# A decoder block on one core: the first batch's context products of the fp8 attention, its input norm and two of its streams issued beside the last scan, and the output weight converted in the seven steps that follow

## The reference

```python
# state space layer, per batch; the norm of (x + this) is the input of the attention
zxbcdt = x @ W_in.T                       # z, x/B/C after a causal convolution, dt
Yd = einsum(M, xs); y = Yd + Yoff + D * xs
yn = rmsnorm(y * silu(z)) * norm_w
x = layernorm(x + yn @ W_out.T)

# fp8 attention layer, per batch
xn = layernorm(x) * ln_w + ln_b
q, qx, k, v = fp8(xn / in_scale) @ wq, wqx, wk, wv       # four "streams"
kx, vx = split(ctx @ w_kv_x)                             # the context products
q, qx, k, kx = per head layer norms
o = concat(softmax(q k) v, softmax(qx kx) vx)
x = layernorm(x + fp8(o / smooth) @ wproj)               # wproj: the output weight
```

## Time and profile before

| | us |
|---|---|
| median of 3 runs | 2132.15 |
| lowest and highest of the 3 | 2131.37, 2134.02 |
| the profiled execution | 2134.4 |
| its span, first to last instruction | 2132.6 |

### The profile page before, as it was taken

The page is one execution under the profiler, slowest core; times in us unless marked ns, Lnnn a source line. Parts: engine busy times, 40 slices in busy tenths (PEclk is TensorE's granted clock), DMA queues, the critical chain, the costliest instruction groups (busy, mean ns, idle before and its releaser), DMA issues.

```text
span 2132.6 us, 34976 instructions
## 1 busy us (share of the span) xinstructions
PE 1977.0 (93%) x9620; PEld 1278.7 (60%) x9620; DVE 1624.9 (76%) x3820; ACT 1392.8 (65%) x5294; POOL 1251.1 (59%) x1540
## 2 busy tenths in 40 slices
PE   7979999999999998799999858999999999999996
PEld 5636666666666666455554425666666666666664
DVE  7855676766776667689899836778888888888887
ACT  3555666666666666356765237777777777777774
POOL 0154445445545443388787924777777777777774
PEclk9999999999999999899999869999999999999998
DMA  6000000000000002100000020000000000000000
GB/s 230 1 18 6 3 4 3 2 2 5 2 2 2 2 0 85 69 3 28 20 21 20 0 74 16 3 4 6 6 6 5 6 5 5 8 5 6 3 3 8
DMA packets 30211, 37.37 MB, mean 18 GB/s; under 512 B 3472, under 2 KB 24464, under 8 KB 29456
## 3 DMA queue, kind: packets, MB, share of 16 engines
q1 hardware_dynamic: 30096, 36.11, 5.1%
HBM read 34.01 MB, written 2.10 MB: 17 GB/s over the span
## 4 chain that ended last, share of the span: by engine, by line
PE 61%; DVE 14%; ACT 11%; POOL 7%; issue 6%; DMA 0%; POOLq 0%; SPq 0%; ACTq 0%; DVEq 0%
PE fa_pJB L2003 5%; PE xa_pJB L736 5%; PE xa_pS L755 5%; PE xa_pO L830 5%; PE xa_pY L867 4%; PE fa_pS L2085 4%; PE xa_pJA L736 3%; PE fa_pO L2028 3%; PE fa_pJA L1983 3%; PE fa_pY L2042 3%; PE fa_pH L2134 3%; PE fa_pJB L1983 2%; POOL ssm_y L1387 2%; PE fa_pH L2101 2%; PE ssm_pX L1445 2%
## 5 line engine op out<-in xcount | busy, mean ns | idle before, releaser
L2160 ACT ACTIVATE fa_qT<-fa_pH,all_fa_head_vec 128x512 f32<-128x512 f32 x128 | 99.9, 780 | 172.0 <-PE fa_pH L2134 172.0
L1933 POOL TENSOR_TENSOR fa_rs<-fa_rs,all_minus_half 128x4 f32<-128x4 f32 x192 | 197.1, 1027 | 15.0
L2169 ACT ACTIVATE fa_pS<-fa_pS,fa_nb 128x128 f32<-128x128 f32 x512 | 183.9, 395 | 6.5 <-DVE fa_nb L2353 6.5
L1930 POOL TENSOR_TENSOR fa_rs<-fa_ms,all_eps5w 128x4 f32<-128x4 f32 x192 | 44.2, 230 | 228.8 <-ACT fa_q_junk L2153 127.0
L1387 POOL TENSOR_TENSOR ssm_y<-ssm_y,ssm_term 128x512 f32<-128x512 f32 x112 | 144.1, 1287 | 55.5 <-DVE ssm_term L1699 52.2
L2085 PEld LDWEIGHTS fa_pS<-fa_kT,fa_qT 128*128 128x128 f32 x1024 | 124.3, 191 | 65.8 <-ACT fa_qT L2160 58.8
L1958 POOL TENSOR_TENSOR fa_cat<-fa_ov,fa_om 128x512 bf16<-128x512 f32 x125 | 150.3, 1203 | 5.1
L2085 PE MATMUL fa_pS<-fa_kT,fa_qT 128*128 128x128 f32 x1024 | 148.2, 288 | 3.0 <-ACT fa_qT L2160 0.9
L1949 POOL TENSOR_TENSOR fa_ov<-fa_ob,fa_om 128x512 f32<-128x512 bf16 x125 | 144.3, 1154 | 0.9 <-DVE fa_om L2301 0.9
L2369 DVE TENSOR_TENSOR fa_qn<-fa_pJA,fa_rs 128x512 f32<-128x512 f32 x128 | 88.4, 691 | 73.4 <-POOL fa_rs L1933 73.3
L682 POOL TENSOR_TENSOR xa_rs<-xa_ms,all_eps 128x4 f32<-128x4 f32 (+1 forms) x65 | 13.1, 202 | 223.1 <-ACT xa_junk L906 223.1
(11 more groups left out here) (340 smaller groups left out, 5802.0 us busy)
## 6 DMA issues: line engine op xcount, KB each, us to landing
all_shared_weights<-in_fa_w SPq DMA_DIRECT2D x12, 512.0 KB, 3.7
fa_cat<-in_fa_wproj SPq DMA_DIRECT2D x8, 512.0 KB, 3.9
all_shared_weights<-in_xa_wq SPq DMA_DIRECT2D x1, 2048.0 KB, 13.8
xa_wo<-in_xa_wo SPq DMA_DIRECT2D x1, 2048.0 KB, 17.9
xa_ctxT<-in_ctxT SPq DMA_DIRECT2D x16, 128.0 KB, 2.1
all_shared_weights<-in_fa_wkvx SPq DMA_DIRECT2D x1, 2048.0 KB, 10.0
fa_ctxT<-in_ctxT SPq DMA_DIRECT2D x16, 128.0 KB, 2.2
out_x<-all_X SPq DMA_DIRECT2D x16, 128.0 KB, 1.7
```

Source lines behind the costliest of these rows:

```text
L1933: pool.tensor_tensor(rs[:, j % 2, cols], rs[:, j % 2, cols], env.mhalf[:, cols], ALU.pow)\
L2169: last = act.activation(four(pS[j % 2])[:, i, :], four(pS[j % 2])[:, i, :], ACT.Exp, bias=nb[:, j % 2, i:i + 1], accum_out=rsum[:, j % 2, ...
```

## The change

What the attention prepares for its batch 1 in steps 0 to 3 is issued from inside the scan, by functions `early(n)` that each engine of `fa` hands to `ssm`:

- PE: the context keys 0 and 1 behind the convolution of batch 16 (m = 15), the key transposes, both context value products and the transposes of `xn` among and behind the levels of batch 16 (m = 16).
- ACT: eight squares at the end of m = 15; `kT` twice, `v` twice and `lnT` at the end of m = 16.
- POOL: one power for both key blocks (128x8 in place of two 128x4) behind its `xd` work of m = 15; the power of `xn` between the sums of levels 3 and 4; the sum of the first stream in m = 17.
- DVE: the input norm and both `kn` between the terms of batch 16; the whole first stream and the second one up to `xm` in m = 17, ahead of the residual of batch 16.

Instead of the norm of batch 16, the first early piece waits for the last use of what the scan's inputs hold (`front_left`); SP loads the context of batch 1 behind the last level of batch 15 and the first two weight chunks behind `front_left`. With m = 0 the steps 0 to 3 of `fa` are gone and 4 to 7 stay (`REST`); the wait for the norm of batch 16 stands behind them, and ACT applies that norm in step 5. The eight weight chunks go to the steps 4, 5, 6 (one each), 7 (two), and 0, 1, 2 of m = 1 (one each), in the order `PROJ`; ACT writes a high part before `qT` and the squares of its step. Buffers are split and laid out anew so that what is used early lies in places that the scan has left.

```diff
+                    if m == B and l == 3:
+                        early(1)
...
                 pool_rms(m - 1)
+                early(2)
                 pool_norm(m - 1)
...
+            if m == B - 1:
+                early(0)
...
+                if m == B and n in (5, 6):
+                    early(n - 4)
...
+            if m == B - 1:
+                early(0)
+            if m == B:
+                early(3)
...
-            if m == B + 1:
-                normalised(m - 1)
-
+            if m >= B - 1:
+                early(m - (B - 1))
...
+        def last_batch_normalised():
+            act.wait_ge(s["shift_done"], now(B, 0))
+            act.activation(shift[:], shift[:], ACT.Copy, scale=-1.0).then_inc(s["shift_signed"], 1)
+            act.wait_ge(s["shift_signed"], now(B, 0))
+            act.activation(env.X[:, B - 1, :], norm.res[:, 0, :], ACT.Identity, bias=shift[:],
+                           scale=norm.rstd[:, 0, :]).then_inc(norm.x_done, 1)
...
+            if m == B + 1:
+                early(3)
             terms(0, 1)
+            if m == B:
+                early(0)
...
+            if m == B:
+                early(1)
...
+            if m == B:
+                early(2)
...
+    def front_left(eng):
+        for n in ("xs_ps", "bc_in", "z_in", "xs_in", "cbd_done", "own_done", "xdt_done"):
+            eng.wait_ge(s[n], now(B, 0))
+        eng.wait_ge(s["dec_late"], of_pair(B))
+        eng.wait_ge(level_ps, now(B - 1, 0, LEVELS, LEVELS - 1))
+        eng.wait_ge(low_done, len(chunks))
...
+    def scan_input_left(eng):
+        eng.wait_ge(level_ps, now(B - 1, 0, LEVELS, LEVELS - 1))
...
+    pJB, pH, pP, pJA = ps("pJB"), ps("pH"), ps("pP"), ps("pJA")
     pS = [ps("pS0"), ps("pS1")]
-    pH, pP, pO, pY = ps("pH"), ps("pP"), ps("pO"), ps("pY")
+    pY, pO = ps("pY"), ps("pO")
...
+    PROJ = [0, 1, 2, 6, 7, 3, 4, 5]
+    REST = range(4, UNITS)
+    PROJ_FIRST = ((), (), (), (), (0,), (1,), (2,), (3, 4))
+    PROJ_SECOND = ((5,), (6,), (7,), (), (), (), (), ())
...
-        steps(0, 0, False, True, False, False)
+        steps(0, 0, False, True, False, False, REST)
+        env.ssm_stage.left(eng)
...
+    def early_of(eng, pieces):
+        def early(n):
+            if n == 0:
+                env.ssm_front_left(eng)
+                eng.wait_ge(env.fa_ready, 1)
+            for piece in pieces[n]:
+                piece()
+        return early
...
-        env.ssm_stage.left(sp)
+        env.ssm_scan_input_left(sp)
         load(1, 1)
+        env.ssm_front_left(sp)
         load_proj(0)
         load_proj(1)
...
+        def first_keys():
+            pool.wait_ge(kk["squared"], at(1, 1, 4))
+            pool.tensor_tensor(rs[:, 0, :], ms[:, 0, :], env.eps5w[:, 0:2 * HG], ALU.add).then_inc(kk["eps"], 2)
+            pool.wait_ge(kk["eps"], at(1, 1, 4))
+            pool.tensor_tensor(rs[:, 0, :], rs[:, 0, :], env.mhalf[:, 0:2 * HG], ALU.pow).then_inc(kk["rstd"], 2)
+        def first_input():
+            pool.wait_ge(s["eps0_done"], at(1, 0, 1))
+            pool.tensor_tensor(rs0[:], mv0[:, 1:2], env.mhalf[:, 0:1], ALU.pow).then_inc(s["rs0_done"], 1)
+        def first_stream():
+            pool.wait_ge(sx["xm_done"], at(1, 0, 4))
+            pool.tensor_tensor(xv[:, STREAMS[0]], xb[:, STREAMS[0]], xm[:, STREAMS[0]], ALU.add)\
+                .then_inc(sx["x_added"], 1)
+        return early_of(pool, [[first_keys], [first_input], [first_stream]]), lambda: sequences(pool, steps, drain)
...
-        env.ssm_stage.left(pe)
-        pe.wait_ge(env.fa_ready, 1)
-        sequences(pe, steps, drain)
+        def context(bank, c, signal):
+            for k in range(KT):
+                last = pe.matmul(bank[:, :], ctxT[:, 1, k, :], w_kvx[:, k, c * 512:(c + 1) * 512],
+                                 start=(k == 0), stop=(k == KT - 1))
+            last.then_inc(signal, 1)
+        def first_products():
+            pe.wait_ge(ctx_in[1], 16)
+            context(pJB, 0, kk["ps"])
+            context(pJA, 1, kk["ps"])
+        def first_keys(n, bank):
+            pe.wait_ge(kk["scaled"], at(1, n, 4))
+            for i in range(HG):
+                last = pe.transpose(bank[:, i * P:(i + 1) * P], kn[:, i, :], env.ident[:])
+            last.then_inc(kk["T_ps"], 1)
+        def first_values(n, bank):
+            context(bank, 2 + n, v_ps)
+        def first_input():
+            pe.wait_ge(s["xn_done"], at(1, 0, 1))
+            pe.wait_ge(kk["T_in"], at(1, 0, 4))
+            for k in range(KT):
+                last = pe.transpose(pH[:, k * P:(k + 1) * P], xn[:, k * P:(k + 1) * P], env.ident[:])
+            last.then_inc(s["xn_ps"], 1)
+        early = early_of(pe, [[first_products], [lambda: first_keys(0, pH)],
+                              [lambda: first_keys(1, pP), lambda: first_values(0, pJB)],
+                              [first_input, lambda: first_values(1, pJA)]])
+        return early, lambda: sequences(pe, steps, drain)
...
-        def steps(m, side, attend, front, back, last_linear):
+        def proj_high(c):
+            act.wait_ge(wp_in[c % 2], 16 * (c // 2 + 1))
+            if c == 5:
+                env.ssm_out_left(act)
+            act.activation(w_proj[:, 0, 4 * PROJ[c]:4 * PROJ[c] + 4, :], wp_raw[:, c % 2], ACT.Copy)\
+                .then_inc(wp_high, 1)
...
+                for c in (PROJ_FIRST[j] if not attend else PROJ_SECOND[j]) if front and not back else ():
+                    proj_high(c)
+                if not attend and front and j == 5:
+                    env.last_batch_normalised()
...
-                if not attend and front:
-                    act.wait_ge(wp_in[j % 2], 16 * (j // 2 + 1))
-                    act.activation(w_proj[:, 0, 4 * j:4 * j + 4, :], wp_raw[:, j % 2], ACT.Copy)\
-                        .then_inc(wp_high, 1)
...
+        def first_squares(n, bank):
+            junk = xq[:, 0, 0:2].rearrange("p s k t -> p (s k) t") if n else k_junk
+            square(kk, bank, junk, ms[:, 0, n * HG:(n + 1) * HG], 1, n, 4)
+        def first_keys(n, bank):
+            act.wait_ge(kk["T_ps"], at(1, n, 4))
+            act.activation(kT[1][:, 0, 4 * n:4 * n + 4, :], four(bank), ACT.Identity, bias=head_vec[:, 7:8],
+                           scale=head_vec[:, 6:7]).then_inc(kk["T_in"], 1)
+        def first_values(n, bank):
+            act.wait_ge(v_ps, at(1, n, 4))
+            act.activation(v[1][:, 0, n * 512:(n + 1) * 512], bank[:, :], ACT.Copy).then_inc(v_in, 1)
+        def first_input():
+            act.wait_ge(s["xn_ps"], at(1, 0, 1))
+            for k in range(KT):
+                last = act.activation(lnT[:, k, :], pH[:, k * P:(k + 1) * P], ACT.Identity,
+                                      bias=vec[:, k, 1:2], scale=vec[:, k, 0:1])
+            last.then_inc(s["lnT_in"], 1)
+        early = early_of(act, [[lambda: first_squares(0, pJB), lambda: first_squares(1, pJA)],
+                               [lambda: first_keys(0, pH), lambda: first_keys(1, pP),
+                                lambda: first_values(0, pJB), first_input, lambda: first_values(1, pJA)], []])
+        return early, lambda: sequences(act, steps)
...
+        def proj_low(c):
+            dve.wait_ge(wp_high, c + 1)
+            to = slice(4 * PROJ[c], 4 * PROJ[c] + 4)
+            dve.tensor_tensor(w_proj[:, 1, to, :], wp_raw[:, c % 2], w_proj[:, 0, to, :], ALU.subtract)\
+                .then_inc(wp_low, 1)
...
+        def first_keys(n, bank):
+            dve.wait_ge(kk["rstd"], at(1, n, 4))
+            dve.wait_ge(kk["T_ps"], at(1, n, 4) - 1)
+            dve.tensor_tensor(kn[:], four(bank), wide(rs[:, 0, n * HG:(n + 1) * HG], HD), ALU.mult)\
+                .then_inc(kk["scaled"], 1)
+        def first_stream():
+            for step in range(4):
+                stream_input(1, 0, step)
+            stream_input(1, 1, 0)
+            dve.wait_ge(sx["x_added"], at(1, 0, 4))
+            dve.tensor_tensor(xq[:, 1, STREAMS[0]], xv[:, STREAMS[0]], xm[:, STREAMS[0]], ALU.subtract)\
+                .then_inc(sx["xq_done"], 1)
+        def second_stream():
+            for step in range(1, 4):
+                stream_input(1, 1, step)
...
-                if not attend and front:
-                    dve.wait_ge(wp_high, j + 1)
-                    dve.tensor_tensor(w_proj[:, 1, 4 * j:4 * j + 4, :], wp_raw[:, j % 2],
-                                      w_proj[:, 0, 4 * j:4 * j + 4, :], ALU.subtract).then_inc(wp_low, 1)
+                for c in (PROJ_FIRST[j] if not attend else PROJ_SECOND[j]) if front and not back else ():
+                    proj_low(c)
...
+        early = early_of(dve, [[lambda: norm_input(1, 0)], [lambda: first_keys(0, pJB)],
+                               [lambda: first_keys(1, pJA), lambda: norm_input(1, 1)], [first_stream, second_stream]])
+        return early, lambda: sequences(dve, steps, drain)
...
-                    env.ssm_stage.gpsimd(pool, tail)
-                    env.fa_stage.gpsimd(pool)
```

(3 more changed lines are left out.)

108 lines of the change are left out of this document (54 added, 54 removed).

## The result

The changed kernel takes 2105.57 us (median of 4 runs, 2103.44 to 2106.76), the kernel before beside it 2131.96 (4 runs). The ratio is 0.9873, with a 95% interval of 0.9856 to 0.9891: faster by 26.4 us or 1.3%. The forecast was 2102.9, so 2.7 us too low, inside its range. The profiled execution took 2105.59 us, its span is 2103.8 against 2132.6.

What follows compares the result with a forecast made beforehand. PE bounds the steady part; in the corner after the scan engines wait for one another. Terms: -32.1 distance, +2.7 POOL, -1.5 clock, +0.9 step 4, +0.8 later steps, so -29.2 from 2132.15 to 2102.9 us, range 2099 to 2109.5.

Steps and rivals of the forecast that it cites:

- shift at the stream: First product from a stream starts at 1240.1 instead of 1270.97, -30.9 us; with half clock on the way -29.4.
- 5: step 4: Step 4, with the residual of batch 16 now due in it, takes 6.0 us instead of 5.14: +0.9.
- Part 1: Two early key products on PE before the levels run at full clock, 1.9 us each; levels 0.5 late, costing nothing.
- Part 2: POOL before the scan's last sums: powers, addition and satisfied waits put the gate 2.7 us later (2.4 to 3.0).
- Part 3: Values and transposes on PE end at 1234.8, before the gate; half clock would hold the gated transposes 2.5 to 3 us.
- Part 4: Gate's end to first product of a stream: about 4.1 us instead of 5.68, through ACT's square, POOL's sum and `xq`.
- Part 6: Steps 5 to 7 and the first steps of m = 1, with the moved weight chunks: +0.8 us in sum (0 to 3).
- A: Rival, 15%: PE at half clock from the context products to the last `ssm_pO`, about 5 us, time 2108.
- B: Rival, 10%: steps 4 to 7 run at full clock and chunk 4 lands in time, -32 to -33 us, 2099.5.
- C: Rival, 8%: weight chunk loads become the path in steps 7, 0 and 1, 3 x 2 us, 2109.
- D: Rival, 3%: an early piece waits for something late and holds the scan; gain 5 to 20 us, 2112 to 2127.
- E: Rival, 3%: new layout of buffers and banks slows the steady loop; at 0.35 us a step 2142.

Runs made afterwards that it cites:

- after: The changed kernel in its first, profiled execution, against the kernel before: 2105.59 us profiled, median 2105.57 us, ratio 0.9873.
- after_again: The changed kernel run again without an edit, against the kernel before: 2104.72 us, ratio 0.9875.
- after_third: The changed kernel run once more without an edit, beside three other kernels on the same chip: 2104.88 us, ratio 0.9869 to the kernel before.
- low_later: The changed kernel with DVE's low part of weight chunk 5 moved a step later, to that of chunk 6: 2102.88 us, ratio 0.9862 to the kernel before.
- no_low_part: The changed kernel with DVE's low parts of the output weight cut to one column, PE's work the same: 2104.03 us, ratio 0.9859 to the kernel before.
- clock_fill: The changed kernel with extra unread products filling idle TensorE: 2104.16 us, ratio 0.9864 to the kernel before.
- experiment 8: The changed kernel with `xn` on DVE between the terms of levels 5 and 6, POOL unchanged: 2102.74 us, ratio 0.9866 to the kernel before.
- experiment 9: The same run as low_later, DVE's low part of chunk 5 a step later in the changed kernel: 2102.88 us, ratio 0.9862.
- Experiment 7: The changed kernel with `xn` behind all sums on POOL and behind the last terms on DVE: 2107.44 us, ratio 0.9878 to the kernel before.
- experiment 11: The changed kernel with the moves of experiment 8 and experiment 9 and the filling products of clock_fill together: 2102.31 us, ratio 0.9857 to the kernel before.
- experiment 2: The changed kernel's buffer layout alone, nothing issued early and one chunk a step, against the kernel before: 2132.25 us, ratio 1.0.

## Why the prediction was right, and where its terms were off

From the taps to step 3 the traces give -27.35 us (after), -29.29 (after_again) and -27.33 (after_third), where the forecast is -29.2. The medians differ by 26.4, 27.4 and 27.3 us. The steps, for after and, in brackets, after_again:

| forecast's part | forecast | measured | |
|---|---|---|---|
| 2: gate | +2.7 | +3.96 (+4.15) | mis-sized |
| 4: gate to stream | 4.9 | 4.78 (4.78) | held |
| shift at the stream | -30.9 | -29.8 (-29.6) | |
| 5: step 4 | +0.9 | +0.71 (+0.72) | held |
| 6: step 5 | +0.1 | -0.08 (-0.07) | held |
| step 6 | -0.8 | -0.33 (-0.32) | |
| step 7 | 0 | -0.41 (-0.89) | |
| step 0 | +1.06 and 0.3 to 0.5 | +2.55 (+0.86) | half clock |

**Part 1.** The choice of the full clock was half wrong. In the nine executions without filling products the first took 2.68 to 3.65 us, and the second 1.88 in six and 2.83 to 2.90 in three (after_again, low_later, no_low_part). The two together took 5.2 to 5.4, where full clock would be 3.7 and half clock 7.3. The wait in front of them was 2.6 to 2.7 us, and the argument put it with those of 1.86 and 2.34, not with 3.98. The first also started 4.50 behind the taps, where 3.84 was taken. The levels started 9.59 behind the taps, between the forecast's two ends (7.5 and 11.1). Of the 1.9 us priced for POOL, 0.75 came (0.91 in after_again, 0.68 in after_third).

**Part 2.** The power (1.66 for 1.64), the addition (0.20) and the power of `xn` (0.55) are as forecast. The 0.2 us for the satisfied waits of `front_left` are in no row: in clock_fill, where POOL waits for no squares, the addition follows the input work without idle time. The first term missing is the 0.75 of part 1. The second is DVE's: "the term of level 5 is still in time for its sum. I count it 0". It was 0.9, because `xn` in front of it took 1.35 us where other rows have it at 0.41; experiment 8, which puts `xn` behind the term, took back 0.6 to 0.8. The Trainium skill, in "GPSIMD Engine Reference" under "Specifications", says that GpSimd shares its SBUF interfaces with VectorE and contends with VectorE instructions in a 2-port mode or with two inputs from SBUF. For the pair of experiment 9 the traces agree: the low part reads two tensors from SBUF, and POOL's power beside it takes 1.46 for 0.55. `xn` reads one tensor and two numbers a row, and no row shows whether it ran in a 2-port mode; that it takes 1.35 for 0.41 beside POOL's sum is told by the rows alone.

**Part 3.** Right: the values ended at 1234.5 and the gated transposes waited for the gate. Experiment 7 shows the other case, at 2.0 us from gate to stream.

**Part 4.** It held, and by the path that it named: POOL waits 1.98 us for ACT's square, its sum takes 0.67 and `xq` 0.43, and only then does PE start. The residual of batch 16 comes later, at 1240.14.

**Part 6.** The wait for chunk 4 and the chunk before `qT` are there. The wait for chunk 4 was put at 0.95 and costs 0 to 0.6. Step 6 gave back 0.3 instead of 0.8. Without the half clock step 0 cost 0.86, where 1.4 to 1.6 was priced; of it 0.5 is the low part's, as forecast in size but by another path: it does not delay the reduction, it slows POOL's power (experiment 9). The 1.7 us that the half clock adds to step 0 in two of the three executions of the changed kernel stood in no part.

For after the shortfall of 1.85 us in the trace is +1.3 (part 2), -0.1, -0.2 (parts 4, 5) and +0.9 (part 6). For after_again +1.45 and -1.2 cancel, so that its -29.29 meets the forecast's -29.2 is luck. What the medians show beyond that, 0.9 us, is within what the start of the taps moves.

**The rivals.** A (half clock up to the last `ssm_pO`) came only in about half of the two key products. B came in step 7 alone, with 0.4 to 0.9: steps 5 and 6 still have half clock, and chunk 4 is waited for. In experiment 11 full clock in step 6 brought nothing, as chunk 4 was then waited for longer. C: in the changed kernel the waits for chunks in step 7 are 0.9 to 1.6 us, none over 2. D and E are false (the table, experiment 2).

The prediction cited "TensorE: Matmul & The Clock Gate" of the Trainium skill for a moment of change that differs between runs of a kernel. The traces agree: behind one wait of 2.05 us, 1.88 four times and about 3.5 twice.

## What to carry to other kernels

A corner in which every engine waits for another is worth what its length is: move whole pieces of the next stage into it, and price the pieces on the engine that sets the pace there, here POOL. Take the duration of a moved DVE or POOL instruction from a row in which the other one of the two is busy, and put it behind, not in front of, the instruction that the other engine waits for. When executions differ by single products at half clock, compare stretches of the traces before medians.

## What the runs showed of the hardware

- VectorE and GpSimd can hold each other up; the one that started second took 2 to 3.5 times as long: `xn` on DVE (128x256) 0.41 us alone, 1.35 and 0.87 beside POOL's 128x512 sum; POOL's 128x1 power 0.55 alone and 1.46 beside DVE's 128x1024 low part, its addition of 128x1 0.67 instead of 0.19. In all four the slowed one ended 0.05 to 0.4 us behind the end of the other (`xn` at 1231.48 and the sum at 1231.34; the power at 1269.68 and the low part at 1269.28), which looks like a wait for the other's end more than a fixed factor. Beside POOL's 128x4 power DVE's `xn` took 0.40 (low_later), so not each pair collides.
- Filling products did not remove the half clock ahead of the gate, they moved it: from the context products (3.54 to 1.96) to the products behind the next wait of 2.41 us (1.10 to 2.05 and 1.89 to 2.62).
- The start of a stretch 1.2 ms into the program differs by 3.7 us between executions whose instructions are the same up to there.
